# Gated stack of four layers on one core: waits on PSUM bank counts in place of separate increments

## The reference

```
for l in 0..3:
    x = x + tanh(g_xattn[l]) * xattn_l(layernorm(x), context)
    x = x + tanh(g_ffn[l])   * ffn_l(layernorm(x))
```

## Time and profile before

| | us |
|---|---|
| median of 3 runs | 653.84 |
| lowest of 3 runs | 653.25 |
| profiled execution, device time | 651.29 |
| its span, first to last instruction | 649.5 |
| PE busy | 442.5 |
| DVE busy | 467.7 |
| ACT busy | 317.2 |
| POOL busy | 231.5 |

### The profile page before, as it was taken

The page is one execution under the profiler, slowest core; times in us unless marked ns, Lnnn a source line. Parts: engine busy times, 40 slices in busy tenths (PEclk is TensorE's granted clock), DMA queues, the critical chain, the costliest instruction groups (busy, mean ns, idle before and its releaser), DMA issues.

```text
span 649.5 us, 11998 instructions
## 1 busy us (share of the span) xinstructions
PE 442.5 (68%) x4134; PEld 294.6 (45%) x4151; DVE 467.7 (72%) x1307; ACT 317.2 (49%) x593; POOL 231.5 (36%) x355
## 2 busy tenths in 40 slices
PE   2565241368997464029998687664889787787996
PEld 2543120235665331025555565442456555564555
DVE  5559899865668676878788878998676888945221
ACT  2477651336654227434657467614565457556100
POOL 4326666528566723601101001443546512110000
PEclk9999555569999658558999869967899988877655
DMA  6730000630000000000000000000000000000000
GB/s 212 160 28 1 1 1 1 195 66 1 1 3 0 2 0 1 0 1 1 2 3 2 2 2 2 3 1 1 2 1 2 1 1 3 2 2 1 1 16 16
DMA packets 26826, 11.95 MB, mean 18 GB/s; under 512 B 15920, under 2 KB 23696, under 8 KB 26768
## 3 DMA queue, kind: packets, MB, share of 16 engines
q1 hardware_dynamic: 26768, 11.20, 7.1%
HBM read 10.67 MB, written 0.52 MB: 17 GB/s over the span
## 4 chain that ended last, share of the span: by engine, by line
DVE 44%; PE 35%; issue 8%; POOL 6%; ACT 4%; DMA 1%; SPq 1%; DVEq 0%; POOLq 0%; ACTq 0%
PE psum L627 10%; DVE qs L1589 6%; PE psum L793 5%; POOL work L594 3%; PE psum L778 3%; PE psum L779 3%; PE psum L780 2%; PE psum L957 2%; DVE stats L1156 2%; DVE z L1165 2%; DVE split L1333 1%; POOL rstd L521 1%; DVE at L1475 1%; DVE work L1460 1%; DVE qs L1169 1%
## 5 line engine op out<-in xcount | busy, mean ns | idle before, releaser
L519 POOL TENSOR_SCALAR vr<-mv 128x1 f32<-128x1 f32 x88 | 19.4, 220 | 227.9 <-DVE mv L1158 227.6
L594 POOL TENSOR_TENSOR work<-work 128x512 f16<-128x512 f32 x64 | 72.5, 1158 | 45.8 <-ACT work L1030 45.8
L1589 DVE TENSOR_REDUCE qs<-psum 128x4 f16<-128x512 f32 x96 | 59.6, 689 | 5.3 <-PE psum L875 5.1
L971 ACT ACTIVATE phase<-psum 128x1024 f16<-128x1024 f16 (+1 forms) x52 | 48.2, 927 | 29.7 <-PE psum L861 14.4
L1460 DVE TENSOR_TENSOR work<-work,psum 128x512 f32<-128x512 f32 x64 | 43.9, 686 | 23.5 <-ACTq L1080 17.0
L1077 ACT ACTIVATE work<-psum 128x512 f32<-128x512 f32 x64 | 38.0, 594 | 36.3 <-PE psum L780 31.2
L1120 ACT ACTIVATE phase<-psum 128x512 f32<-128x512 f32 x96 | 49.8, 603 | 9.9 <-PE psum L900 8.6
L778 PE MATMUL psum<-zTh,split 128*128 128x512 f16 x128 | 51.8, 405 | 2.1 <-DVE work L1460 1.7
L521 POOL TENSOR_TENSOR rstd<-vr,mhalf 128x1 f32<-128x1 f32 x88 | 50.4, 573 | 7.3
L793 PE MATMUL psum<-wout,work 128*128 128x128 f16 x768 | 49.8, 225 | 3.9 <-POOL work L594 1.8
L793 PEld LDWEIGHTS psum<-wout,work 128*128 128x128 f16 x768 | 46.8, 101 | 10.1 <-POOL work L594 3.7
(11 more groups left out here) (339 smaller groups left out, 1081.6 us busy)
## 6 DMA issues: line engine op xcount, KB each, us to landing
stage_f<-in_L_ffn_W_in SPq DMA_DIRECT2D x1, 2048.0 KB, 10.0
stage_f<-in_L_ffn_w SPq DMA_DIRECT2D x1, 2048.0 KB, 8.6
x<-in_x SPq DMA_DIRECT2D x1, 512.0 KB, 4.3
c<-in_ctx SPq DMA_DIRECT2D x1, 512.0 KB, 5.5
w<-in_L_ffn_W SPq DMA_DIRECT2D x2, 256.0 KB
out<-x SPq DMA_DIRECT2D x8, 64.0 KB, 1.6
rows<-in_L_xattn_b SPq DMA_DIRECT2D x4, 64.0 KB, 7.9
rows<-in_L_xattn_bo SPq DMA_DIRECT2D x3, 64.0 KB, 7.9
```

The lines of the kernel that those rows point to most:

```text
L594: ch.do(pool.tensor_tensor(hidl[:, n % 2, k, :], act[:, n % 2, k, :], hidh[:, n % 2, k, :], ALU.subtract), sem("hid_low"))
L971: ch.do(A(out, view(u), ACT.Copy), banks.freed(stage, b, name))
L1589: ch.do(v.tensor_reduce(groups(qs[:, b, :, 3 * DA:3 * DA + 1], 4)[:, j], u, AX.X, ALU.max, negate=True), free_of(stage, b, f"s{j}"))
```

## The change

`Banks` gets two methods that only wait: `filled` (for `full`) and `emptied` (for `free`), both with the count of one use of a bank. Wherever an engine waited for a named semaphore that was raised behind the return of a bank, it now waits for the bank's own count, and the sync and the increment go. Where an engine waited to hear that a result of PE had been used or copied, it waits for the count of full of the matmul that reads or writes it. Waits for a running number (zT of the fourth batch, say) become waits for each batch's own bank. In `normalise` the wait for `stats_ready` goes. f0_t and f2_t keep a sync between the copy to zT and the copy to zTh. In x0_score PE waits for the copy of am first and for that of qk only before the scores. No operation is added, taken out or moved. The core of the diff:

```diff
-    def get(self, eng, *key):
+    def filled(self, eng, *key):
         k, turn = self.place[key]
         eng.wait_ge(self.full[k], turn + 1)
-        return self.psum[:, k * BANK:(k + 1) * BANK]
+    def emptied(self, eng, *key):
+        k, turn = self.place[key]
+        eng.wait_ge(self.free[k], turn + 1)
+    def get(self, eng, *key):
+        self.filled(eng, *key)
+        return self.tile(*key)
...
-                    pe.wait_ge(sem("qk0_T"), b + 1)
-                    pe.wait_ge(sem("am_T"), b + 1)
+                    banks.emptied(pe, "x0_stack", b, "am")
                     us = [banks.take(pe, stage, b, f"e{g}") for g in range(2)]
...
+                    banks.emptied(pe, "x0_stack", b, "qk")
                     us = [banks.take(pe, stage, b, f"s{g}") for g in range(2)]
...
-                    pe.wait_ge(sem(stage[:2] + "_zT"), own[-1] + 1)
                     u = banks.take(pe, stage, b, "logit")
                     for i, b_ in enumerate(own):
+                        banks.emptied(pe, stage[:2] + "_t", b_, "u")
...
-                    pe.wait_ge(sem(m + "_stacks"), b + 1)
+                    if m == "c":
+                        pe.wait_ge(sem("c_stacks"), b + 1)
+                    else:
+                        banks.emptied(pe, m + "_kv", b, "qkv")
                     if m == "b":
-                        pe.wait_ge(sem("b_qs"), b + 1)
+                        banks.emptied(pe, "b_q", b, "q")
...
-                    pe.wait_ge(sem(m + "_qkT"), b + 1)
+                    banks.emptied(pe, m + "_stack", b, "qk")
...
-                    pe.wait_ge(sem("f3_zT"), HALF * (b + 1))
+                    for bb in range(HALF * b, HALF * (b + 1)):
+                        banks.emptied(pe, "f3_t", bb, "u")
...
-                    pe.wait_ge(sem("h3_gated"), 4 * (b + 1))
-                    pe.wait_ge(sem("h3_ready"), 5 * (b + 1))
+                    for k in range(4):
+                        banks.emptied(pe, "f3_gate", b, f"gate{k}")
+                    banks.emptied(pe, "f3_up", b, "h4")
...
-            def copy_free(stage, b, name, out, view, signal):
+            def copy_free(stage, b, name, out, view):
                 u = banks.get(act_, stage, b, name)
                 ch.do(A(out, view(u), ACT.Copy), banks.freed(stage, b, name))
-                ch.sync()
-                act_.sem_inc(signal, 1)
...
                     if n >= 2:
-                        act_.wait_ge(sem("hid_used"), n - 1)
+                        banks.filled(act_, *list(down_turn)[n - 2], "u")
                     for k in range(2):
-                        act_.wait_ge(sem("hid_ready"), 2 * n + k + 1)
+                        banks.emptied(act_, stage[:2] + "_up", b, f"g{k}")
...
                     if b >= 2:
-                        act_.wait_ge(sem("cc_ready"), 2 * (b - 1))
+                        banks.filled(act_, "x0_score", b - 2, "s1")
...
                         ch.do(A(dec[:, b % 2, j, :, :], u.rearrange("p (h q) -> p h q", h=4), ACT.Exp), banks.freed(stage, b, f"e{j}"))
-                        ch.sync()
-                        act_.sem_inc(sem("dec_ready"), 1)
...
                     if b >= 2:
-                        act_.wait_ge(sem("cc_used"), b - 1)
+                        banks.filled(act_, "x0_value", b - 2, "u")
...
             def normalise(stage, out, src, b, signal):
                 turn = norm_turn[NORM_OF[stage], b]
-                dve.wait_ge(sem("stats_ready"), turn)
                 dve.wait_ge(sem("rstd_ready"), turn)
...
                     if b >= 2:
-                        dve.wait_ge(sem("x0_stacked"), b - 1)
+                        banks.filled(dve, "x0_stack", b - 2, "qk")
...
                     for j in range(2):
-                        dve.wait_ge(sem("dec_ready"), 2 * b + j + 1)
+                        banks.emptied(dve, stage, b, f"e{j}")
                         u = get(stage, b, f"s{j}").rearrange("p (h q) -> p h q", h=4)
...
-                        ch.sync()
-                        dve.sem_inc(sem("cc_ready"), 1)
...
-                        dve.wait_ge(sem("act_ready"), 2 * n + k + 1)
+                        banks.emptied(dve, stage, b, f"a{k}")
                         u = get(stage, b, f"g{k}")
                         ch.do(tt(act[:, n % 2, k, :], act[:, n % 2, k, :], u, ALU.mult), free_of(stage, b, f"g{k}"))
-                        ch.sync()
-                        dve.sem_inc(sem("hid_ready"), 1)
...
-                    dve.sem_inc(sem("hid_used"), 1)
...
-                        dve.wait_ge(sem("f1_zT"), 4 * (g + 1))
+                        for bb in range(4 * g, 4 * g + 4):
+                            banks.emptied(dve, "f1_t", bb, "u")
...
                         split_v(b, v_, f)
-                        ch.sync()
-                        dve.sem_inc(sem(m + "_stacks"), 1)
```

More of the change, by code:

```diff
@@ L669, in _ @@
                         u0 = banks.take(pe, "x0_gate", 0, "gates")
-                        pe.wait_ge(sem("wT_ready"), 3)
+                        for i in range(2):
+                            banks.emptied(pe, "setup", 0, f"ctx{i}")
                         pe.wait_ge(sem("w_kv_ready"), 1)
@@ L682, in _ @@
                     banks.fill(one(u[:, 0:NB * H0], tri[:, :], gf[:, :, :]), stage, 0, "csum")
-                    pe.wait_ge(sem("a_ready"), 1)
+                    banks.emptied(pe, stage, 0, "csum")
                     u = banks.take(pe, stage, 0, "at")
@@ L743, in _ @@
                     w = {"f0_route": wg0, "f2_route": routerT, "f3_route": wg3}[stage]
-                    if stage == "f2_route":
-                        pe.wait_ge(sem("router_T"), 1)
+                    if stage == "f2_route" and b == 0:
+                        banks.emptied(pe, "router", 0, "u")
                     if stage == "f3_route":
@@ L816, in _ @@
                     pe.wait_ge(sem("xq_ready"), g + 1)
-                    pe.wait_ge(sem("w8_T"), 3)
+                    if cch == 0 and g == 0:
+                        for i in range(3):
+                            banks.emptied(pe, "w8", i, "u")
                     for i, name in enumerate(("up", "gate")):
@@ L832, in _ @@
                             loaded(pe, "l2")
[L833 removed]
+                        banks.emptied(pe, "x2_t", b, "u")
                         last = one(u[:, 0:3 * D], zT[:, b, :], wA[:, :, :].rearrange("p i d -> p (i d)"))
@@ L839, in _ @@
                             loaded(pe, "l3")
-                        pe.wait_ge(sem("x3_zT"), b + 1)
+                        banks.emptied(pe, "x3_t", b, "u")
                         one(u[:, 0:D], zT[:, b, :], wC[:, 0, :])
@@ L848, in _ @@
                 elif stage == "b_q":
-                    pe.wait_ge(sem("b_qt_T"), b + 1)
+                    banks.emptied(pe, "b_qt", b, "t")
                     u = banks.take(pe, stage, b, "q")
@@ L881, in _ @@
                     for j in range(4):
-                        pe.wait_ge(*banks.freed(m + "_max", b, f"s{j}"))
+                        banks.emptied(pe, m + "_max", b, f"s{j}")
                     u = as16(banks.take(pe, stage, b, "q"))
@@ L890, in _ @@
                     n = 3 * DA + 1
-                    pe.wait_ge(sem(m + "_q2T"), b + 1)
+                    banks.emptied(pe, m + "_again", b, "q")
                     for pair in ((0, 1), (2, 3)):
@@ L925, in _ @@
                     m = stage[0]
-                    pe.wait_ge(sem(m + "_wt_T"), b + 1)
+                    banks.emptied(pe, m + "_wt", b, "t")
                     u = banks.take(pe, stage, b, "wo")
@@ L929, in _ @@
                 elif stage == "b_f":
-                    pe.wait_ge(sem("b_ft_T"), b + 1)
+                    banks.emptied(pe, "b_ft", b, "t")
                     u = banks.take(pe, stage, b, "f")
@@ L943, in _ @@
                 elif stage == "f3_gate":
-                    pe.wait_ge(sem("gT_ready"), b + 1)
+                    banks.emptied(pe, "f3_gt", b, "gt")
                     pe.wait_ge(sem("sel_ready"), 1)
@@ L1035, in _ @@
                     ch.do(A(gb[:, :, :], ga[:, :, :], ACT.Ln, bias=1.0), sem("softplus"))
-                    act_.wait_ge(sem("md_ready"), 1)
+                    banks.emptied(act_, stage, 0, "m")
                     ch.do(A(floor[:, :, :], gb[:, :, :], ACT.Exp, scale=-1.0), sem("floor_ready"))
@@ L1078, in _ @@
                               banks.freed(stage, b, f"a{k}"))
-                        ch.sync()
-                        act_.sem_inc(sem("act_ready"), 1)
                 elif stage == "f1_up":
@@ L1131, in _ @@
                 elif stage in atT:
-                    copy_free(stage, b, "t", atT[stage][:, :], lambda u: u[:, 0:P], sem(stage + "_T"))
+                    copy_free(stage, b, "t", atT[stage][:, :], lambda u: u[:, 0:P])
                 elif stage == "f3_up":
@@ L1317, in _ @@
                     ch.sync()
-                    dve.sem_inc(sem("md_ready"), 1)
                     for src, st, o in ((ga, ast, 0), (mm, mst, 3)):
```

(13 more changed lines are left out.)

52 lines of the change are left out of this document (23 added, 29 removed).

## The result

Four runs of the changed kernel have a median of 633.44 us (631.82 to 634.26), beside 653.55 us for the kernel before (652.74 to 653.84 in three of its four runs; the fourth took 1997.44 us and is left out of the ratio). The ratio is 0.9693, 95% interval 0.9665 to 0.9722: faster by 3.1%. The forecast of 643.0 us moved the right way and by half of it, and its range of 635 to 652 us does not hold the time.

The account below looks back on a forecast made before the run. No engine fills the span: DVE bounds x0, PE the f0 experts and f3's end, both alternate in attention. Chain terms of 14.4 us, discounted by stage to 10.8, gave 653.8 - 10.8 = 643.0 us, range 635 to 652.

Parts of the forecast that it names:

- The price of a site: Each DVE instruction losing its pause on the path: 0.14 us of sync and increment plus 0.09 overlap gives 0.23.
- Parts 1 and 2: Same engine goes on: 40 DVE sites 9.2 us, 21 second waits 1.5; on ACT eight sites 1.5, one increment 0.1.
- The discounts by stage: Chain sums cut: x0 4.2 to 2.7 us, expert stages 4.1 to 3.0, attention 4.0 to 3.2, rest 2.1 to 1.9.
- rival C: In x0 DVE's copy precedes POOL's subtraction, or PE keeps high clock: 4.2 + 5.6 in x0, 635.9 us; chance 0.21.
- Parts 3 to 5: Increments in front of work 1.1 us, stats wait in normalise 0.6, hops to another engine 0.5.
- The added waits: Single waits becoming one per batch or bank, about 20 on PE and DVE: 0.1 us, 1.4 if all bare.
- TensorE's clock: In f3, 596 to 644 us, PE bound mostly at half clock; clock changes may shift, about 3 us either sign.
- The step from the trace to the median: Profiled 651.29 us less 10.8 gives 640.5; the median is 2.5 above, so 653.8 - 10.8 = 643.0.
- A: Pauses cost nothing by themselves, DVE may empty its pipeline anyway: only 2.2 us saved, 651.6 us; chance 0.10.
- B: DVE and POOL meet more often in x0: two more per batch, 14.4 us lost against 10.8 won, 657.4; chance 0.07.
- D: Waits on a bank's count could come later than the old ones: time stays 653.8 us; chance 0.02.
- What would show it: Products step 0.6 us, rstd to z 0.03, f0 experts 65, issue about 6%, x0 over 1, attention over 2 shorter.

Follow-up runs that it names:

- pauses: Changed kernel with sync and increment put back at every place but nine increments, nobody waiting on the semaphore: 651.7 us, ratio 0.997 to the kernel before.
- inc_only: Changed kernel with only the increments put back, no wait for the own instruction in front of them: 634.34 us, ratio 0.9711 to the kernel before.
- pause_att: Changed kernel with sync and increment put back in the attention stages alone: 639.51 us, ratio 0.9796 to the kernel before.
- pause_act: Changed kernel with sync and increment put back at ACT's places in all stages, none of DVE's: 637.52 us, ratio 0.9758 to the kernel before.
- pause_x0: Changed kernel with sync and increment put back in x0_stack, x0_score and x0_value alone: 637.68 us, ratio 0.9768 to the kernel before.
- pause_exp: Changed kernel with sync and increment put back in f0_up, f0_down, f2_up and f2_down alone: 638.01 us, ratio 0.9759 to the kernel before.
- att_fill: Kernel before with three more matmuls of unread result in b_wt, where PE waits for DVE: 653.46 us, ratio 1.0027 to the kernel before.
- sync_only: Changed kernel with only the wait for the own instruction put back, no increment: 645.37 us, ratio 0.9889 to the kernel before.
- tail_fill: Changed kernel with 24 added matmuls of unread result in f3_gate and f3_down: 643.38 us, ratio 0.9865 to the kernel before.

## Why the prediction was right in its mechanism and half the size

**The price of a site (0.23 us): right.** It was read from a gap of 0.14 us and an overlap of 0.09 that no gap shows; the traces of `pauses` and `inc_only` give 0.43 less 0.20 = 0.23. The second wait of 0.07 us behind a pause is right as well: 0.31 between the products is 0.12 + 0.19, and 0.19 is the 0.11 of the increment alone and 0.08 more.

**Which part of it costs: put together wrongly.** The prediction laid the 0.14 us to sync and increment together without parting them. The runs part them: half belongs to the sync, and the increment costs only behind a sync. For the kernels' sum this changes nothing; for what to take away next it is the point.

**Parts 1 and 2, the number of sites: the first step that failed.** Sites were counted on the one chain that ended last in the kernel before: in attention 13 on DVE, 3.3 us with their second waits. Laid side by side, DVE's instructions of both traces come closer at 19 of the 24 sites of a and b (16 of L1579, 8 of L1584), on that chain or not: by 0.23 us at eleven, by 0.30 or 0.31 at six, where a second wait stood behind the pause, and by 0.37 and 0.68 at two, where another wait got shorter too. At the other five DVE waits for another engine anyway, and they give 0.00 to 0.08. Together that is 5.6 of the 7.0 us, and `pause_att` measures 6.1, where the sum along the chain had 4.0. I read it so: these stages are a ring through DVE, PE and ACT that turns once a batch, and the chain that ends last passes in each turn through one engine's part of it where two are almost equally late; once one is shorter, the site of the other is on the next chain. That is argued, not shown. ACT's part is undersized too: eight sites at 0.19 gave 1.5 us, `pause_act` costs 4.1 us (runs from 0.9 to 5.4). Of this 3.2 us stand in b's stretch below, where its trace has a lower clock as well, so ACT's pauses alone may be worth less.

**The discounts by stage: the second step that failed.** "There another thing stands beside the chain" cut x0 from 4.2 to 2.7 us, the experts from 4.1 to 3.0 and attention from 4.0 to 3.2. Measured were 4.2 (`pause_x0`; 4.3 in the windows), 4.6 (`pause_exp`, uncertain) and 6.1. The rest, 1.9 in the sum, is 5.2 (20.1 less 14.9): 3.4 of it are pauses outside these stages or scatter, and no run parts it. For x0 the timeline tells why. The changed kernel, one batch, DVE and POOL (compare):
```profile
64.63 1.28 DVE L1333 SCALAR_TENSOR_TENSOR split<-psum,split 128x512 f32<-128x512 f32 x2
65.83 0.28 DVE L1173 CAST phase<-z 128x256 f16<-128x256 f32 x1
66.15 0.29 DVE L1262 TENSOR_TENSOR phase<-z,phase 128x128 f16<-128x128 f32 x1
66.19 1.26 POOL L583 TENSOR_TENSOR phase<-split,phase 128x512 f16<-128x512 f32 x1
66.36 1.18 DVE L1169 TENSOR_SCALAR z<-x,mv,rstd 128x128 f32<-128x128 f32 x1
...
68.24 1.19 POOL L589 TENSOR_TENSOR split<-stage_f,split 128x512 f16<-128x512 f32 x1
68.46 1.12 DVE L1380 TENSOR_TENSOR t<-t,rows 128x128 f32<-128x128 f32 x1
69.61 0.64 DVE L1382 SCALAR_TENSOR_TENSOR x<-t,tg,x 128x128 f32<-128x128 f32 x1
70.29 0.29 DVE L1161 BATCH_NORM_STATS2 stats<-x 128x6 f32<-128x128 f32 x1
```
DVE's cast (L1169 of before, L1173 now) gets in ahead of POOL's subtraction and takes 0.28 us instead of 1.12, as rival C had it. But the z behind it now falls into that subtraction, 1.18 us where it is 0.45 in the kernel before, and further down L1380 takes the place of L1379 inside POOL's next one. From the cast's start to the statistics it is 4.46 us (65.83 to 70.29), and in the timeline of the kernel before 4.52 (59.34, to 63.86). In the two batches behind it the stretch takes 4.46 us again, where it took 5.64 and 4.15: over the three batches 13.4 us instead of 14.3. The collisions move and their sum changes little. So the discount for them was wrong, and so was the bonus of 5.6 us in C: what was won is the pauses, whole (8 x 0.31 + 8 x 0.24 = 4.4 us). A batch takes 9.64 us (60.65 to 70.29, from statistics to statistics) instead of 10.32 (59.34 to 69.66, from cast to cast).

**Parts 3 to 5, not contradicted.** Increments in front of work, the stats wait and the hops were 1.1 + 0.6 + 0.5 us; what the change gives beside pauses and increments is 652.6 less 651.7 = 0.9 us (ratio 0.997, up to 3.8 us by the interval) and the increments alone 0.9. The added waits at 0.1 us: nothing in these runs speaks against it.

**TensorE's clock, kept out of the sum with 3 us: nothing in x0 and f3, about 1 us in b.** In f3 the clock is 0.57 before and after, and the stretch 48.0 and 47.8 us long; the first eight matmuls of f3_gate take 3.64 us instead of the 4.04 of the earlier trace rows and the second eight 6.84 as before. In x0 the clock rose from 0.65 to 1.00, but that is neither the change's doing nor worth anything. `inc_only`, which is as fast as the changed kernel, has the low clock there and needs 81.7 us all the same:
```profile
40.80:122.50 81.70, 32.04 (x349) 21.92 (x346) 75.79 (x196) 40.83 (x89) 52.60 (x64) 0.65 0.11 35
```
The mean granted clock of an execution varies by itself: in 44 executions of the kernel before on four chips it lies between 0.769 and 0.866, and the 18 at 0.85 or more have a median of 652.8 us, the other 26 one of 652.5. The bound in x0 is DVE, and the gain is the pauses'.

In b the same work was cut out of several traces, from the splits of one batch to the output of another, about 25 us long. The changed kernel:
```profile
361.70:387.00 25.30, 21.16 (x358) 16.40 (x356) 23.12 (x68) 18.76 (x40) 3.12 (x8) 0.90 0.01 3
```
The kernel before, its pauses in it:
```profile
374.30:402.90 28.60, 23.39 (x358) 18.09 (x356) 23.56 (x67) 19.77 (x40) 3.12 (x8) 0.81 0.01 2
```
`pause_act`, with ACT's pauses in it:
```profile
364.50:393.10 28.60, 24.02 (x359) 18.63 (x356) 23.38 (x67) 19.77 (x39) 3.13 (x8) 0.80 0.01 2
```
`pauses`, with all pauses in it and a high clock:
```profile
372.90:400.40 27.50, 22.07 (x358) 16.96 (x356) 23.50 (x69) 20.05 (x40) 3.12 (x8) 0.90 0.01 2
```
`att_fill`, all pauses in it, a high clock and twelve added matmuls:
```profile
375.90:403.80 27.90, 23.73 (x370) 17.56 (x367) 23.50 (x68) 19.96 (x40) 3.12 (x8) 0.92 0.01 2
```
`pause_x0`, no pause in this stretch:
```profile
367.30:393.80 26.50, 21.74 (x358) 16.77 (x356) 23.30 (x68) 18.92 (x40) 3.13 (x8) 0.91 0.01 2
```
With all pauses the stretch takes 27.5 us at a clock of 0.90 and 28.6 at 0.81; without any it takes 25.3 to 26.5, always at 0.90 or more. `pause_att` has 29.3 us at 0.79, and `sync_only`, with half of each pause, 28.5 at 0.81, as long as the kernel before. So of the difference of 3.3 us the pauses make about 2.2 (the five DVE sites in it give 1.7) and the clock about 1.1, which agrees with the 1.3 us read in `att_fill`. Both are one trace against another, and traces of the same work lie up to 1.2 us apart here. Why the clock falls for longer in some executions than in others stays open; pauses alone don't decide it, since `pauses` has them all and the high clock.

**The step from the trace to the median.** The prediction took 10.8 us from a profiled execution of 651.29 and added the 2.5 us by which the median stood above it. That median was the higher of two ordinary runs, since the third took 1997.44 us; on the four chips of the later runs the kernel before has medians of 652.0 to 654.4. The changed kernel's profiled execution stands 0.6 below its median. 640.5 against 632.84 is a miss of 7.7 us, 643.0 against 633.44 one of 9.6; the 1.9 between are not the argument's but those of one execution taken for the middle of many.

**The rivals.** A (the pauses cost nothing, 651.6) is fallen: the syncs alone cost 12 us. The Trainium skill's rule (VectorE: DVE Perf Modes, "The DRAIN you can't avoid"), by which a semaphore behind each of eight copies costs nothing, agrees with `inc_only`, where more semaphores are raised at no cost, and does not agree with `sync_only`, where the engine also waits for one. B (slower, more meetings) and D (no effect) did not come. C's time, 635.9, was the nearest, but that is luck: its main reason, 5.6 us of meetings avoided, is not what happened, and its other one, a high clock kept, is worth about 1 us in b and nothing in x0.

**What would show it.** The products step by 0.60, z follows rstd by 0.03 us, the experts keep their time, x0 and attention are shorter by more than the bounds named: all held. The share of "issue" fell from 8 to 6% as forecast, but it is 6% in `pauses` too, at 651.7 us, so it proves nothing: with the overlap lost, a pause shows mostly as a longer share of DVE (46% there) and not as "issue".

## What to carry to other kernels

Price a wait for the engine's own result by the step from start to start of two like instructions, with it and without, not by the gap: 0.12 us for the sync, 0.11 for an increment behind it, 0.07 for each further wait. Let the instruction itself raise what others wait for, put independent work between producer and reader so that the sync is met when it is reached, and count in a ring of engines all sites of the stage and not those of the one chain that ended last. Don't discount a shift for collisions with POOL without following the next ones: here they moved, and over three batches their sum fell by 0.9 us. And read what a clock is worth from two traces of the same work: it varied from one execution to the next with no change in the code.

## What the runs showed that was not expected

- An increment by the queue is free as long as no sync stands before it: 634.3 us with nearly all of them back against 633.4, and 6.3 us for the same ones behind syncs.
- A DVE instruction with one SBUF tensor as input waits for POOL as well: z (L1169, 128x128, f32 from SBUF) took 1.18 us inside POOL's L583 and 0.31 to 0.35 in most other places (283 us into the changed kernel it stands with 0.36 in the chain). The Trainium skill has this as an exclusive lock on a shared pair of ports (SBUF — State Buffer, "SBUF: two separate sides"); the trace agrees, though it does not show in which mode the instruction ran.
- PE's granted clock stayed at 0.50 from 592 us on in `tail_fill` although PE had been busy without a pause for the 14 us before, the last 4 of them at 0.53 already, with the added bf16 matmuls among its work (624 ns each in the second stretch).
- Twenty microseconds of 653 went with 500 instructions (11,998 in the kernel before, 11,498 now) that the page's chain puts at "DVEq 0%" and "ACTq 0%": their price stands in "issue" and in the lengths of the instructions behind them.
